# Rotated queries and keys stored by half in blocks, so that each row loads as 8 KB

## What is computed

```python
B, S, D, H, HD = 4, 512, 128, 16, 8          # 77 context tokens
for i in range(6):
    xn = adaln(x, noise_emb, n1_w[i], n1_b[i])
    q, k, v = split(xn @ qkv_w[i].T)
    q, k = rope(q), rope(k)                   # 16 heads of 8 features
    x = x + attn(q, k, v, src_mask) @ so_w[i].T
    xn = adaln(x, noise_emb, n2_w[i], n2_b[i])
    q = rope(xn @ cq_w[i].T); k = rope(context @ ck_w[i].T); v = context @ cv_w[i].T
    x = x + attn(q, k, v, ctx_mask) @ co_w[i].T
    xn = adaln(x, noise_emb, n3_w[i], n3_b[i])
    x = x + gelu(xn @ f1_w[i].T + f1_b[i]) @ f2_w[i].T + f2_b[i]

def rope(x):                                  # per head, halves x1, x2
    return concat([x1 * cos - x2 * sin, x1 * sin + x2 * cos])
def attn(q, k, v, mask):                      # scores / sqrt(8), -inf where masked, softmax
    ...
```

## Time and profile before

| | us |
|---|---|
| median of three runs | 2217.02 |
| lowest and highest | 2212.71, 2217.53 |
| profiled execution, its own time | 2213.04 |
| its span in the trace | 2211.2 |

### The profile page before, as it was taken

The page is one execution under the profiler, slowest core; times in us unless marked ns, Lnnn a source line. Parts: engine busy times, 40 slices in busy tenths (PEclk is TensorE's granted clock), DMA queues, the critical chain, the costliest instruction groups (busy, mean ns, idle before and its releaser), DMA issues.

```text
span 2211.2 us, 40093 instructions
## 1 busy us (share of the span) xinstructions
PE 1802.6 (82%) x13138; PEld 767.3 (35%) x13138; DVE 1723.1 (78%) x4125; ACT 1517.0 (69%) x2808; POOL 1035.1 (47%) x1506
## 2 busy tenths in 40 slices
PE   4564185278999999999999999999999999999662
PEld 2332174122333333333333333333333333333231
DVE  6766111588899888998888987889988889888777
ACT  2443031156888888888888887888888888889553
POOL 2443712824454555454554554554545545444532
PEclk9766598569999999999999999999999999999785
DMA  3001122322423343423533325333244232432100
GB/s 101 1 0 38 56 86 76 85 52 69 96 66 67 88 101 79 92 59 70 108 82 83 79 55 112 86 68 88 53 106 94 71 81 68 90 86 59 30 2 20
DMA packets 153736, 155.11 MB, mean 70 GB/s; under 512 B 32247, under 2 KB 137523, under 8 KB 153523
## 3 DMA queue, kind: packets, MB, share of 16 engines
q1 hardware_dynamic: 151487, 148.34, 28.8%
q0 software_dynamic: 2048, 4.20, 0.7%
HBM read 82.15 MB, written 67.85 MB: 68 GB/s over the span
## 4 chain that ended last, share of the span: by engine, by line
PE 55%; DVE 10%; DMA 9%; POOL 6%; ACT 5%; issue 3%; SPq 2%; POOLq 0%; DVEq 0%; ACTq 0%
PE ps L1357 14%; DMA q<-scratch_queries 8%; PE ps L1310 7%; PE ps L1321 6%; DVE smax L1878 4%; PE ps L1459 4%; PE ps L1469 4%; ACT big L1586 4%; PE ps L1368 3%; PE ps L1433 2%; PE ps L600 2%; PE ps L610 2%; PE ps L1393 2%; PE ps L1344 2%; PE ps L1332 1%
## 5 line engine op out<-in xcount | busy, mean ns | idle before, releaser
L1586 ACT ACTIVATE big<-ps 128x512 f32<-128x512 f32 x1920 | 1009.6, 613 | 214.9 <-PE ps L1321 204.6
L1878 DVE TENSOR_REDUCE smax<-ps 128x1 f32<-128x512 f32 x1536 | 966.7, 684 | 175.8 <-PE ps L1310 123.3
L1357 PE MATMUL ps<-big,vaug 128*32 128x512 f32 x3072 | 430.4, 634 | 2.3 <-ACT xnT L1594 1.2
L1310 PE MATMUL ps<-k,q 49*128 49x512 bf16 x1536 | 294.7, 394 | 80.9 <-DMA q<-scratch_queries 56.1
L1321 PE MATMUL ps<-q,k 52*128 52x512 bf16 x1536 | 291.1, 392 | 9.2 <-DVE smax L1878 3.3
L1310 PEld LDWEIGHTS ps<-k,q 49*128 49x128 bf16 x1536 | 76.1, 94 | 314.4 <-DVE smax L1878 153.1
L1789 POOL CAST mparts<-smax 128x16 bf16<-128x16 f32 x96 | 19.2, 200 | 324.4 <-DVE smax L1878 324.4
L1886 DVE TENSOR_REDUCE maxima<-ps 128x4 f32<-128x308 f32 x384 | 157.2, 469 | 9.4 <-PE ps L1344 5.9
L1321 PEld LDWEIGHTS ps<-q,k 52*128 52x128 bf16 x1536 | 78.9, 94 | 215.5 <-issue 65.4
L1775 POOL TENSOR_TENSOR rot<-rot,cs 128x512 f32<-128x512 f32 x72 | 92.0, 1277 | 103.3 <-DVE rot L1897 103.3
L1780 POOL TENSOR_TENSOR hat<-rot,rparts 128x512 f32<-128x512 f32 x72 | 82.6, 1161 | 70.6 <-ACT rparts L1634 70.6
(11 more groups left out here) (312 smaller groups left out, 2938.2 us busy)
## 6 DMA issues: line engine op xcount, KB each, us to landing
k<-scratch_keys SPq DMA_DIRECT2D x48, 384.0 KB
q<-scratch_queries SPq DMA_DIRECT2D x48, 384.0 KB, 8.1
cq<-scratch_cross_queries SPq DMA_DIRECT2D x48, 384.0 KB, 6.0
scratch_keys<-rparts SPq DMA_DIRECT2D x24, 384.0 KB, 2.5
scratch_queries<-rparts SPq DMA_DIRECT2D x24, 384.0 KB
scratch_cross_queries<-rparts SPq DMA_DIRECT2D x24, 384.0 KB
scratch_keys<-rparts SPq DMA_DIRECT2D x24, 256.0 KB, 2.2
scratch_queries<-rparts SPq DMA_DIRECT2D x24, 256.0 KB
```

The source lines that it names most:

```text
L1310: last = nc.tensor.matmul(out[u], m.q6[rows, v % 2, 2 * g + pr, qt * P:(qt + 1) * P], m.k6[rows, v % 2, 2 * g + pr, :], start=True, stop=True)
L1357: last = nc.tensor.matmul(m.ps[32 * j:32 * j + 32, pv_bank, :], of_head(m.vaug, v % 2 * TB + kt, g, j), of_quad("self", q)[:, j, :], start ...
L1586: nc.scalar.activation(of_quad(kind, p // 2)[:, p % 2 * 2 + u, :], bank("exp" if kind == "self" else "cross exp", p, u), ACT.Exp, scale=sc ...
L1878: nc.vector.tensor_reduce(m.smax[:, n % 2, qt, u, pr:pr + 1], bank("max", i, u), AX.X, ALU.max).then_inc(s_read["self"], 1)
```

## The change

The scratch tensors get another form: (2 halves, 48 rows, 8 pairs, 512 tokens), a row being one feature of one product for all pairs of one half, 8 KB in one piece. For keys there are 56 rows: the mask row, the three constant rows and four more rows of mask, written once in the slot stage; the mask row is no longer loaded by itself. To make this possible with stores whose partition runs over whole lanes, the columns of the projections and the rotary tables are permuted on the host (`features`), so that lanes 0 to 63 are one half, each lane a (feature, pair).

- A load of queries or keys is still two DMAs, one per half, but with one 8 KB piece per partition; 56 partitions for keys, 48 for queries. `load_rows` takes the place of `load_queries` and `load_keys`, at the place of the former; it waits for both stores and then issues keys, queries, keys, queries.
- A store is split in two, since the halves lie apart: each DMA reads 64 partitions and writes pieces of 1 KB. Before, the stores of queries wrote pieces of 3, 2 and 1 KB from 128 partitions, those of keys 1 KB.
- `piece_landed`, `rows_landed` and `PIECES` (1) only count semaphores. All other places in the orders are the old ones. The mask used by DVE's shuffle (`OTHER_HALF`) pairs lanes 8 apart and not 4.

```diff
@@ slot stage
+            for u in range(2):
+                for first, last in ((ROW_MASK, ROW_SHIFT), (ROWS_ALL, ROWS_STORED)):
+                    sp.dma_start(a["keys"][:, u, first:last].rearrange("b r i n -> b (r i) n"),
+                                 m.negmask[:].unsqueeze(1).to_broadcast([B, (last - first) * PAIRS, S])).then_inc(shift_out, 16)
+                for b in range(B):
+                    sp.dma_start(a["keys"][b, u, ROW_SHIFT:ROWS_ALL], m.shift_rows[:]).then_inc(shift_out, 16)
-                for i in range(2):
-                    sp.dma_start(m.k6[shift:shift + 3, i], m.shift_rows[:]).then_inc(shift_out, 16)
@@ stores
-    sp.dma_start(dst[:, 0:3, :], parts[:, 0:3, :]).then_inc(stored, 16)
-    sp.dma_start(dst[:, 3:5, :], parts[:, 0:2, :]).then_inc(stored, 16)
-    sp.dma_start(dst[:, 5:6, :], parts[:, 0:1, :]).then_inc(stored, 16)
+    for lo, hi in ((0, 3), (3, 5), (5, 6)):
+        for u in range(2):
+            sp.dma_start(planes(dst[u], lo, hi), parts[u * ROW_BLOCK:(u + 1) * ROW_BLOCK, 0:hi - lo, :]).then_inc(stored, 16)
...
-    sp.dma_start(dst[:, lo:hi, :], parts[:, stage:stage + 1, :].to_broadcast([P, hi - lo, parts.shape[2]])).then_inc(stored, 16)
+    for u in range(2):
+        part = parts[u * ROW_BLOCK:(u + 1) * ROW_BLOCK, stage:stage + 1, :]
+        sp.dma_start(planes(dst[u], lo, hi), part.to_broadcast([ROW_BLOCK, hi - lo, parts.shape[2]])).then_inc(stored, 16)
+def planes(rows, lo, hi):
+    return rows[lo * HD:hi * HD].rearrange("(c r) i n -> (r i) c n", r=HD)
@@ places
-    "SP load queries": (-32643,),
-    "SP load keys": (-32960,),
+    "SP load rows": (-32643,),
@@ loads
+            def load_rows(j):
+                v, k, b, i = j // PIECES, j % PIECES, j // PIECES % B, j // PIECES % 2
+                if k == 0:
+                    sp.wait_ge(x_stored["query"], STORED * (v + 1))
+                    sp.wait_ge(x_stored["key"], STORED * (v + 1))
+                if v >= 2:
+                    sp.wait_ge(scores["self"], PER_VISIT * (v - 2) + PER_VISIT // PIECES * (k + 1))
...
+                for u in range(2):
+                    at = u * ROW_BLOCK
+                    sp.dma_start(m.k6[at:at + ROWS_STORED, i, lo:hi].rearrange("p i n -> p (i n)"),
+                                 a["keys"][b, u, :, lo:hi].rearrange("p i n -> p (i n)")).then_inc(loaded[i][k % 2], 16)
+                    sp.dma_start(m.q6[at:at + ROW_MASK, i, lo:hi].rearrange("p i n -> p (i n)"),
+                                 a["queries"][b, u, :, lo:hi].rearrange("p i n -> p (i n)")).then_inc(loaded[i][k % 2], 16)
@@ load_cross
-                src = a["cross_queries"][v % B].rearrange("(i u r) c n -> u (r c) i n", u=2, r=HD)
                 for u in range(2):
-                    sp.dma_start(m.cq[u * ROW_BLOCK:u * ROW_BLOCK + ROW_MASK], src[u]).then_inc(c_loaded, 16)
+                    sp.dma_start(m.cq[u * ROW_BLOCK:u * ROW_BLOCK + ROW_MASK].rearrange("p i n -> p (i n)"),
+                                 a["cross_queries"][v % B, u].rearrange("p i n -> p (i n)")).then_inc(c_loaded, 16)
@@ max_scores
-                if i % PER_VISIT == 0:
-                    pe.wait_ge(q_loaded[v % 2], 32 * (v // 2 + 1))
-                    pe.wait_ge(k_loaded[v % 2], 64 * (v // 2 + 1))
+                if i % (PER_VISIT // PIECES) == 0:
+                    j = i // (PER_VISIT // PIECES)
+                    pe.wait_ge(loaded[v % 2][j % PIECES % 2], piece_landed(j))
@@ scratch
-"queries": ((B, P, PRODUCTS, S), BF16), "keys": ((B, P, PRODUCTS, S), BF16), "cross_queries": ((B, P, PRODUCTS, S), BF16), "ctx_keys": ((P, PRODUCTS, NC_ALL), BF16)
+"queries": ((B, 2, ROW_MASK, PAIRS, S), BF16), "keys": ((B, 2, ROWS_STORED, PAIRS, S), BF16), "cross_queries": ((B, 2, ROW_MASK, PAIRS, S), BF16), "ctx_keys": ((2, ROW_MASK, PAIRS, NC_ALL), BF16)
```

More of the change, by code:

```diff
@@ L755, in store_query_parts, with features @@
 def store_query_parts(sp, dst, parts, stored):
-    sp.dma_start(dst[:, 0:3, :], parts[:, 0:3, :]).then_inc(stored, 16)
-    sp.dma_start(dst[:, 3:5, :], parts[:, 0:2, :]).then_inc(stored, 16)
-    sp.dma_start(dst[:, 5:6, :], parts[:, 0:1, :]).then_inc(stored, 16)
+    for lo, hi in ((0, 3), (3, 5), (5, 6)):
+        for u in range(2):
+            sp.dma_start(planes(dst[u], lo, hi), parts[u * ROW_BLOCK:(u + 1) * ROW_BLOCK, 0:hi - lo, :]).then_inc(stored, 16)
 def store_key_part(sp, dst, parts, stage, stored):
     lo, hi = ((0, 3), (3, 5), (5, 6))[stage]
-    sp.dma_start(dst[:, lo:hi, :], parts[:, stage:stage + 1, :].to_broadcast([P, hi - lo, parts.shape[2]])).then_inc(stored, 16)
+    for u in range(2):
[3 more added lines that the diff above has]
+    return rows[lo * HD:hi * HD].rearrange("(c r) i n -> (r i) c n", r=HD)
+def features():
+    halves, pairs = HD // 2, PAIRS
+    lane = np.arange(D)
+    u, low, high, i = lane // ROW_BLOCK, lane // (2 * pairs) % halves, lane // pairs % 2, lane % pairs
+    return (2 * i + u) * HD + high * halves + low
 VISITS = LAYERS * B
-OTHER_HALF = [lane ^ (HD // 2) for lane in range(32)]
+OTHER_HALF = [lane ^ PAIRS for lane in range(32)]
+PIECES = 1
+PIECE = PAIRS // PIECES
 PER_UNIT = 2 * TB
@@ L776 @@
 UNIT_PAIRS = GROUPS // 2
+STORED = 16 * 6
 PARTS = {
@@ L781 @@
         "first query", "less query", "second query", "third query", "product key", "rope key", "rotate key", "first key", "less key",
-        "second key", "third key", "store query", "store key 0", "store key 1", "store key 2", "load queries", "load keys", "values",
+        "second key", "third key", "store query", "store key 0", "store key 1", "store key 2", "load rows", "values",
         "copy values", "weights next", "gain next"),
@@ L1022, in layers, with piece_landed, rows_landed @@
     w_sem = sems("weights", SECTION_GROUPS)
-    q_loaded, k_loaded, m_rows = [sems(n, range(2)) for n in ("queries_loaded", "keys_loaded", "shift_rows")]
+    def piece_landed(j):
+        return 64 * ((PIECES + 1) // 2 * (j // PIECES // 2) + j % PIECES // 2 + 1)
+    def rows_landed(sp, v):
+        for k in range(min(PIECES, 2)):
+            sp.wait_ge(loaded[v % 2][k], 64 * ((PIECES + 1) // 2) * (v // 2 + 1))
+    m_rows = sems("shift_rows", range(2))
+    loaded = [sems(f"rows_loaded{i}_", range(min(PIECES, 2))) for i in range(2)]
     c_loaded, kc_loaded, c_m_rows = sem("cross_queries_loaded"), sem("context_keys_loaded"), sem("cross_shift_rows")
@@ L1266, in _ @@
                     load_cross(i)
[L1267 to L1270, removed]
+                for i in due("SP load rows", now):
+                    load_rows(i)
                 for i in due("SP load context", now):
@@ L1664, in round_block @@
                 if b == 0:
-                    act.wait_ge(x_stored["context"], 48 * LAYERS)
+                    act.wait_ge(x_stored["context"], STORED * LAYERS)
                 else:
@@ L2338, in layer_cols @@
         return np.concatenate(vecs).T
-    cos, sin = rotary_tables()
+    cos, sin = (table[turned] for table in rotary_tables())
     got = {
```

37 lines of the change are left out of this document (19 added, 18 removed).

## The result

| | before | after |
|---|---|---|
| median, us | 2214.86 (4 runs) | 2330.74 (4 runs, 2328.43 to 2331.04) |
| span of the profiled execution | 2211.2 | 2326.7 |
| ratio to before | | 1.0525, interval 1.05 to 1.055 |

The account below looks back on a forecast made before the run. Bound: stores then loads through DRAM, in a row, with PE waiting in 21 of 24 visits. 21 x (2.5 - 0.2) = 48 us, cross queries 2, clock 9, say + 60 on 2213.04: 2273, stated as 2275; range 2190 to 2325.

Parts of the forecast that it names:

- Step 2: Loads of keys and queries, 8 KB pieces and 8 more key rows: - 0.2 us per visit, bounds - 5.0 and + 0.8.
- Step 1: Stores split by half, more issues and slower data before the load: + 2.5 us per visit, bounds + 1.9 and + 3.8.
- Step 6: Longer PE waits give more time at the lower clock, low time up by a third: 9 us, bounds 0 and 27.
- Steps 3, 4 and 5: SP's dropped mask DMAs: nothing; cross queries' later landing: 2 us for all; slot stage's and context keys' extra DMAs: nothing.
- A: Rival: long pieces are what the loads lacked; loads take 4.7 us, the wait all but vanishes, 2150 us; chance 0.17.
- B: Rival: halves' loads overlap better or pieces help half-way, 2.5 us shorter, paying for the stores: 2205 to 2225; chance 0.07.
- C: Rival: stores also run at 162 GB/s and the keys' 8 rows count in full, 2340 us; chance 0.09.

Follow-up runs that it names:

- e3: Changed kernel with its four loads reordered to keys, keys, queries, queries, so that halves alternate: 2305.76 us, 1.0416 of before.
- e9: Changed kernel with each store whole again, one DMA of 128 partitions, and loads in alternating halves: 2216.48 us, 0.9996 of before.
- e2: Changed kernel with keys and queries each loaded by one DMA over 128 partitions, filler rows included: 2206.38 us, 0.9972 of before.
- e8: Changed kernel with loads over 128 partitions, keys and queries each cut into two DMAs with 4 KB pieces: 2247.22 us, 1.0127 of before.
- e5: Kernel before, old scratch form and loads, only each store split into two of 64 partitions: 2307.31 us, 1.0405 of before.
- e4: Changed kernel with scratch rows padded per pair, so loads come in 1 KB pieces, same partitions and order: 2355.79 us, 1.0645 of before.
- e6: Kernel before with queries stored in stages, first and second part ahead of the keys' second store: 2166.93 us, 0.9776 of before.
- e1: Changed kernel with the halves' rows alternating in scratch and lanes permuted, so each store is one DMA of 128 partitions: 2261.64 us, 1.0219.

## Why the prediction was wrong

Of the 56 us between the forecast (2275) and the time, the loads are the largest part: 21 x 1.4 = 29 us. The stores are 21 x 1.1 = 23, and the clock is 11; the waits themselves add up to 5 less than the medians do, and the 2 taken for the cross queries did not show.

**What bounds the kernel** held: the stores and the loads between the last part and PE's first use are in a row, PE's arrival didn't move (13.7 us after the second key store in every kernel), and each microsecond there came out as wait, 21 times. The slot stage cost nothing: the first visit's first key store is issued at 415.6 us, before it was 416.3.

**Step 2, the loads, had the wrong sign: + 0.9 us of data and + 0.3 from the last packet to PE's start measured, - 0.2 taken.** The order of the four loads had changed, from alternating halves to two on one half and then two on the other. The step put that at nothing, without a reason. e3 gives it 1.5 us; without it (e9 and e3 against before) the data would have been 0.5 to 0.6 us shorter, nearer to what I wrote. What I said of their bound was right: e2 and e8 show 356 to 438 GB/s over 128 partitions once the data flows. The Trainium skill ("SBUF — State Buffer", "Door 1: The DMA port swizzle") gives 8 of 16 ports to one half, and the rates agree with it: 131 to 197 GB/s on halves. The Trainium skill ("SBUF — State Buffer", "Can I just issue two DMAs to hit both halves?") puts two DMAs on two halves at only 6% more bandwidth than one. That compares another thing than e3 does, where the order of four DMAs took the data from 10.9 to 9.3 us, 14% less; the order counted for more here than that figure suggests.

**Step 1, the stores, was too small: + 3.6 us measured, + 2.5 taken.** It was near the upper bound (3.8), for another reason. I had bounded the issues by their old pace, 2.8 us for five more, and let the data rate decide. The issues didn't keep their pace: from the second key store on, five took 2.8 us before and ten take 6.6 us in the changed kernel (6.7 in e5), 3.7 us more; in the median of the keys' stores half a store costs SP more than a whole one (0.61 against 0.39 us). And I had let the data catch up with the issues by 0.9 us; the load follows the last of them by 1.5 us where it was 1.8, so it caught up by 0.3. The DMA engines are partly idle there, as shown above. With the engines busy for 0.93 and more, half-partition stores ran at 249 to 252 GB/s, at which the 1.18 MB would be through in an estimated 4.7 us; the data would not have decided. The Trainium skill's rule against two transfers to disjoint halves ("DMA: Bandwidth & Descriptors", "Rules for kernel authors") gave the right warning. The trace agrees in that the halves' rate stays under the 346 to 382 GB/s of whole stores; but the price was paid in issues.

**Step 6, the clock, was too small: 9 us taken, about 20 measured** (116 less the 96 of the wait). The granted clock over most visits fell from 0.98 to 0.94, three times the low share in place of the one third more that I took. The clock's records agree with the size: PE was busy at the lower level for 137 us where it was 95, and half of the 42 us more is 21. Much of the added low time falls into the waits, where PE has no work to lose: low time grew by 116 us in the visits, PE's work in it by 42. Steps 3, 4 and 5 held: no wait for `cq`'s load from scratch appears in either kernel.

The sum with what was measured: 21 x (3.6 + 0.9 + 0.3) = 101 from the medians, 96 by the wait itself, and 20 for the clock: 116 us. The 0.3 us between the last packet and PE's start (0.9 for 0.6) was not taken apart.

**The rivals.** A (long pieces free the loads) is refuted by the profile after and by e4. (Its sum was also off by 2: 2213 - 68 is 2145 and not 2147.) B needed about 235 GB/s in the loads; they show 163. C (2340) came nearest to the time, and its condition, a rate of the stores under 170 GB/s, was nearly met on average: 171 over 884.40 to 891.40. But its mechanism, stores that move as slowly as the loads do, was not: with the engines busy they run at 249 to 252. Where C has 4.6 us a visit, 3.8 for the stores' data and 0.8 for more rows, the runs show issues and the order of loads; that the time comes near is luck. It had 0.09; I gave the step's own upper end too little weight.

What stays open: why the issue of a half store takes longer on SP than that of a whole one. It is not the number of partitions as such, for loads of 48 and 56 partitions are issued in 0.32 to 0.51 us (medians by place) in both kernels. No run changed the clock alone.

## What to carry to other kernels

Where a transfer is on the path, count its DMAs at the price that the changed form will have, not the old one: cutting stores in halves cost more issue time than the loads' longer rows could give back. Look at the order of the transfers too: the same four loads took 1.5 us longer when both of one half came first. Before shortening a load by longer pieces, look at how many partitions it fills; covering all 128 with filler moved 23% more bytes in 55% of the time. And take what can go earlier off the path first: storing the ready parts early took 52 us off the kernel before, the new form of scratch alone nothing (e9).

## What the runs showed of the hardware

- An issue of a store from 64 partitions took SP 0.61 us in the median, whether of 192, 128 or 64 KB, and 0.61 us also for the cross queries, before whose first store the DMA engines are idle for the microsecond in the median visit. One from 128 partitions took 0.34 to 0.39 us there (medians by stage). Of the five stores from the second key store on it took 0.38, 0.41, 0.45, 0.72 and 0.65 us (medians, kernel before), so that the last ones of a crowded stretch are dearer; with two of them taken out (e6) the last took 0.34.
- Loads of 48 to 56 partitions: 10.9 us when two on the same half follow each other, 9.3 us when halves alternate, for 1.70 MB.
- One microsecond of wait on PE costs more than itself, by the clock: over the kernels above, 96 us more wait gave 116 us, 28 us less wait gave 52 us less, 49 us less gave 74 us less. (The kernel before differed by up to 6 us between the sets of runs.) It is no fixed price per microsecond: 32 us more wait (e1) already brought PE's work at the lower clock from 95 to 133 us, 96 us more only to 137. Half the change of that work comes within 8 us of what each time moved beyond its waits. In the changed kernel's visit above PE stood still from 897.04, the granted clock was 0.50 from 900 on, and the first pair of matmuls after the wait took 0.61 us in place of 0.39.
